# Attention experts: eight keys and values projected first, and five passes instead of six

## The reference

```
def _expert(x, Wqkv, bqkv, Wo, bo, g1, be1, W1, bf1, W2, bf2, g2, be2):
    q, k, v = split(x @ Wqkv.T + bqkv)          # 8 heads of 64
    attn = softmax((q / 8) @ k.T, axis=-1)      # over all 128 nodes
    ctx = (attn @ v) @ Wo.T + bo
    x = layernorm(x + ctx, g1, be1)
    h = gelu(x @ W1.T + bf1)                    # 512 -> 64
    h = gelu(h @ W2.T + bf2)                    # 64 -> 512
    return layernorm(x + h, g2, be2)

probs = softmax((x @ gate_Wk.T + gate_bk) @ expert_queries.T * D ** -0.5)
gated = probs of the top 2 of 8 experts, over their sum + 1e-9, 0 for the others
out = sum over e of gated[:, e] * _expert(x, e)
```

## Time and profile before

| | |
|---|---|
| three timed runs | 439.18, 439.82, 439.83 us, median 439.82 |
| the profiled execution | 439.57 us, of which the span is 437.8 |
| PE busy | 408.1 us, 93% of the span |
| DVE, ACT, POOL busy | 47%, 30%, 9% |
| attention experts, from the first q matmul to the sum written to x | 167.2 to 319.0 us |

### The profile page before, as it was taken

One profiled execution on the slowest core, in us unless ns is written; L12 is line 12 of the kernel. 1 busy time (PEld: TensorE's weight loads), 2 busy tenths in 40 slices (PEclk: granted clock), 3 DMA queues, 4 the chain that ended last, 5 costly groups with the idle time before them and its releaser, 6 DMA issues.

```text
span 437.8 us, 7601 instructions
## 1 busy us (share of the span) xinstructions
PE 408.1 (93%) x2811; PEld 308.5 (70%) x2811; DVE 207.6 (47%) x598; ACT 131.3 (30%) x382; POOL 40.9 (9%) x80
## 2 busy tenths in 40 slices
PE   7998999896499989999999999998999999999996
PEld 6698655885098789797685669656788995393482
DVE  5743554555994254562745547557442621111102
ACT  2313322414562112351533235342112231222130
POOL 4000010011453011001000010001010000000000
PEclk9999999999769999999999999999999999999999
DMA  8999569322002200999999999337200499999900
GB/s 288 394 426 354 217 248 398 145 98 96 0 2 97 97 0 2 370 393 422 416 320 313 358 422 306 95 122 310 104 0 0 192 418 425 421 418 421 390 5 24
DMA packets 19494, 104.31 MB, mean 238 GB/s; under 512 B 3538, under 2 KB 5458, under 8 KB 7809
## 3 DMA queue, kind: packets, MB, share of 16 engines
q1 hardware_dynamic: 19168, 103.81, 61.7%
q10 hardware_dynamic: 288, 0.02, 0.1%
HBM read 103.56 MB, written 0.26 MB: 237 GB/s over the span
## 4 chain that ended last, share of the span: by engine, by line
PE 52%; issue 4%; DVE 2%; DMA 1%; ACT 1%; POOL 0%; SPq 0%; POOLq 0%; DVEq 0%; ACTq 0%
PE ps L1186 9%; PE ps L1172 8%; PE ps L1855 6%; PE ps L1589 6%; PE ps L1578 3%; PE ps L1569 3%; PE ps L1672 3%; DMA ew<-in_l_wq 1%; PE ps L1206 1%; PE ps L1693 1%; PE ps L1921 1%; PE ps L1702 1%; PE ps L1197 1%; PE ps L1216 1%; PE ps L1155 1%
## 5 line engine op out<-in xcount | busy, mean ns | idle before, releaser
L1155 PE MATMUL ps<-ident 128*128 128x128 f32 x352 | 48.8, 292 | 2.8 <-POOL ident L664 2.8
L1155 PEld LDWEIGHTS ps<-ident 128*128 128x128 f32 x352 | 46.3, 207 | 5.0 <-POOL ident L664 2.8
L1186 PEld LDWEIGHTS ps<-y_t,ew 128*128 128x128 f32 x352 | 39.9, 192 | 1.7 <-issue 1.7
L1186 PE MATMUL ps<-y_t,ew 128*128 128x128 f32 x352 | 40.2, 275 | 0.0
L1172 PE MATMUL ps<-ew,y_t 128*128 128x512 f32 x72 | 32.7, 597 | 0.0
L1589 PE MATMUL ps<-y_t,ew 128*128 128x128 f32 x224 | 27.5, 277 | 0.0
L1589 PEld LDWEIGHTS ps<-y_t,ew 128*128 128x128 f32 x224 | 26.1, 192 | 0.8 <-issue 0.7
L813 ACT ACTIVATE prob_store<-ps,nmax_s 128x128 f32<-128x128 f32 x56 | 19.7, 384 | 14.5 <-DVE nmax_s L2047 14.5
L1172 PEld LDWEIGHTS ps<-ew,y_t 128*128 128x128 f32 x72 | 13.0, 190 | 13.5 <-issue 13.3
L2655 DVE SCALAR_TENSOR_TENSOR t<-prob_store 128x512 f32<-128x512 f32 x6 | 4.2, 692 | 36.4 <-ACT prob_store L1089 20.4
L749 POOL TENSOR_TENSOR ln_rstd<-ln_mv,minus_half 128x1 f32<-128x1 f32 x12 | 6.6, 549 | 127.7 <-DVE ln_mv L2409 127.7
(11 more groups left out here) (529 smaller groups left out, 759.4 us busy)
## 6 DMA issues: line engine op xcount, KB each, us to landing
ew<-in_l_w SPq DMA_DIRECT2D x20, 1024.0 KB, 21.5
dense<-in_l_w SPq DMA_DIRECT2D x12, 1024.0 KB, 21.1
ew<-in_l_wv SPq DMA_DIRECT2D x8, 1024.0 KB, 14.8
ew<-in_l_wk SPq DMA_DIRECT2D x7, 1024.0 KB, 15.3
ew<-in_l_wq SPq DMA_DIRECT2D x6, 1024.0 KB, 11.8
erows<-in_l_rows SPq DMA_DIRECT2D x4, 1280.0 KB, 12.8
ew<-in_l_wo SPq DMA_DIRECT2D x5, 1024.0 KB, 14.8
ew<-in_gqa_wq SPq DMA_DIRECT2D x3, 1024.0 KB, 10.5
```

The lines of the kernel that those rows point to most:

```text
L1155: pe.matmul(ps[:, b, 3 * P:4 * P], ident[:], ident[:], start=True, stop=True)
L1186: last = pe.matmul(ps[:, b, m * n:(m + 1) * n], w[:, c, (first + m) * P:(first + m + 1) * P], in_t[:, c, 0:n], start=(c == 0), stop=(c == ...
```

## The change

All eight keys come first, then all eight values, each in the order of the experts' own numbers, so none of them waits for the ranking. Their results stay in `k_all` and `v_all` (four slots of `dense`), and GpSimd copies those of a pass's experts into the tiles that the matmuls read (`keys_copy`, `values_copy`). All eight experts are ranked. Ranks 0 and 1 have passes of their own, the first and the last; ranks 2 and 7 share one in groups of 96 and 32 slots, ranks 3 and 4, and 5 and 6, share one each in halves. [...]

With no projections of keys and values left beside the passes, `beside_pair` holds the steps of pass t, the gather, the q and its turning for pass t+2, and the scores. The value's bias moves behind the attention (`v_bias` now adds it to the transposed context, since the weights of a row sum to one), and that copy out of PSUM moves from ScalarE to VectorE. The key's bias moves from VectorE to ScalarE. The last two passes are interleaved by hand. GCN's weights no longer load into `dense` ahead of the stage, but into `ew` during the passes.

```
-L2_STEPS = ((0,), (1,), (2, 3), (4,), (5, 6), (7,))
-L2_RANKS = (None, 0, 3, 4, 1, 5, 6, 2)
+L2_STEPS = ((0,), (1, 2), (3, 4), (5, 6), (7,))
+L2_RANKS = (0, 2, 7, 3, 4, 5, 6, 1)
+L2_PAIRS = (1, 2, 3)
+L2_SPANS = {1: (slice(0, 96), slice(96, P)), 2: (slice(0, 64), slice(64, P)), 3: (slice(0, 64), slice(64, P))}
+L2_GROUPS = {1: ((0, 0, 64), (0, 64, 96), (1, 96, P)), 2: ((0, 0, 64), (1, 64, P)), 3: ((0, 0, 64), (1, 64, P))}
...
             def load_l2_rows(t, experts):
+                for r, e in zip(L2_SPANS[t] if t in L2_PAIRS else (slice(0, P),), experts):
+                    sp.dma_start(erows[r, t % 2], A["l2_rows"][e].rearrange("(a r) n -> a r n", a=1)
+                                 .broadcast_to([r.stop - r.start, 4, D])).then_inc(sig(f"l2_rows_landed{t % 2}"), 16)
...
             sp.wait_ge(*at("l2_expert_added", 1))
+            load_l2_rows(2, (e3, e4))
...
+            def keys_copy(t):
+                pool.wait_ge(*at("l2_k_ready", E))
+                if t:
+                    pool.wait_ge(*at("l2_scored", 2 * t))
+                for a, p in enumerate(L2_STEPS[t]):
+                    pool.tensor_copy(keys_of[a].rearrange("p c n -> p (c n)"),
+                                     k_all[:, bass.ds(experts[p], 1), :].rearrange("p e n -> p (e n)")) \
+                        .then_inc(sig("l2_k_copied"), 1)
+
+            def values_copy(t):
+                pool.wait_ge(*at("l2_v_ready", E))
+                if t:
+                    pool.wait_ge(*at("l2_attended", t))
...
+            keys_copy(0)
+            keys_copy(1)
+            values_copy(0)
+
+            keys_copy(2)
+            values_copy(1)
+            inner_norm(0, 1)
...
+            def on_groups(t, b, in_t, kind, columns=slice(0, D), started=False):
+
+                for c in range(CH):
+                    for a, first, end in L2_GROUPS[t]:
+                        last = pe.matmul(ps[first:end, b, 0:columns.stop - columns.start], in_t[:, c, first:end],
+                                         l2_w(kind, L2_STEPS[t][a])[:, c, columns],
+                                         start=(c == 0 and not started), stop=(c == CH - 1))
+                return last
...
             def beside_pair(t):
 
-                first, second = L2_STEPS[t + 2]
-                step_attend(t, 7)
+                step_attend(t, 1)
                 gather_rows(t + 2)
                 step_o(t)
-                expert_k(first, range(CH))
                 pair_q(t + 2)
                 x1_transposes(t)
-                expert_k(second, (0, 1))
+                turn_q(t + 2)
                 step_h1(t)
-                turn_q(t + 2)
-                expert_k(second, (2, 3))
+                probs_t(t + 1)
                 step_h2(t)
-                probs_t(t + 1)
-                step_v(t + 1)
                 step_scores(t + 2)
...
+            for e in range(2, 7):
+                expert_k(e)
+            expert_q(0)
+            expert_k(7)
+            expert_v(0)
             step_scores(0)
+            expert_v(1)
+            gather_rows(1)
+            expert_v(2)
+            pair_q(1)
+            expert_v(3)
+            turn_q(1)
             probs_t(0)
+            for e in range(4, E):
+                expert_v(e)
             step_scores(1)
+
             beside_pair(0)
-            beside_dense(1)
-            beside_pair(2)
-            beside_dense(3)
+            beside_pair(1)
...
+            step_attend(2, 1)
+            keep_clock(2, times=2)
+            step_o(2)
+            expert_q(4)
+            x1_transposes(2)
+            turn_scatter()
+            step_h1(2)
+            probs_t(3)
+            step_h2(2)
+            step_scores(4)
+
+            step_attend(3, 1)
+            keep_clock(2, times=2)
+            step_o(3)
+            keep_clock(2, times=8)
+            probs_t(4)
+            x1_transposes(3)
+            step_attend(4, 0)
+            step_h1(3)
+            step_o(4, (0,))
+            step_h2(3)
+            step_o(4, (1,))
```

More of the change, by code:

```diff
@@ L1631, in step_scores @@
                 for g in range(4):
-                    for a, r in enumerate(token_half):
-                        for rows, keys in zip(token_half, (qk_t[:, CH:], k_second)):
-                            last = pe.matmul(ps[rows, 3 + a, g * P:(g + 1) * P], qk_t[r, g, rows], keys[r, g, :],
-                                             start=True, stop=True)
+                    for h, r in enumerate(token_half):
+                        for a, first, end in L2_GROUPS[t]:
+                            last = pe.matmul(ps[first:end, 3 + h, g * P:(g + 1) * P], qk_t[r, g, first:end],
+                                             keys_of[a][r, g, :], start=True, stop=True)
                         if g == 3:
@@ L1651, in step_attend @@
                 pe.wait_ge(*at("l2_prob_t_ready1", t + 1))
-                for rows, values in zip(token_half, (v, v_second)):
+                for tokens, values in zip(L2_SPANS[t], values_of):
                     for g in range(4):
@@ L1778, in _ @@
+            step_h1(2)
[13 more added lines that the diff above has]
+            step_o(4, (1,))
             pe.wait_ge(*at("l2_scatter_ready", 1))
             pe.matmul(bank(2), gated_t[:], be2[:], start=True, stop=False)
-            pe.matmul(bank(2), scatter[:, 0:P], pair_rows[0], start=False, stop=False)
@@ L1781, in _ @@
-            keep_clock(1, times=6)
-            pe.wait_ge(*at("l2_expert_added", 5))
-            pe.matmul(bank(2), scatter[:, P:2 * P], pair_rows[1], start=False, stop=True).then_inc(sig("l2_mixed"), 1)
-            x1_transposes(5)
+            for k in range(2):
+                pe.matmul(bank(2), scatter[:, k * P:(k + 1) * P], pair_rows[k], start=False, stop=False)
+            keep_clock(1, times=4)
+            x1_transposes(4)
             keep_clock(1, times=3)
-            step_h1(5)
@@ L1787, in _ @@
-            keep_clock(1, times=2)
-            step_h2(5)
+            step_h1(4)
+            pe.wait_ge(*at("l2_expert_added", LAST))
+            pe.matmul(bank(2), scatter[:, 2 * P:3 * P], pair_rows[2], start=False, stop=True).then_inc(sig("l2_mixed"), 1)
+            step_h2(4)
             gcn_out = ((4, 5), (6, 7), (0, 3))
@@ L2402, in statistics @@
-            def statistics(rows):
-                settle()
-                dve.bn_stats(ln_st[:, 0:6], rows[:])
-                aggregate(ln_st[:])
+                dve.wait_ge(*at("l2_attended", t + 1))
+                for tokens, p in zip(L2_SPANS[t] if t in L2_PAIRS else (slice(0, P),), L2_STEPS[t]):
+                    last = dve.tensor_tensor(ctx_t[:, :, tokens], bank_chunks(0 if t == LAST else 1)[:, :, tokens],
+                                             bqk[:, bass.ds(experts[p] * 12 + 2 * CH, CH)].unsqueeze(2)
+                                             .broadcast_to([P, CH, tokens.stop - tokens.start]), ALU.add)
@@ L2407, in aggregate @@
+                last.then_inc(sig("l2_ctx_t_ready"), 1)
+            rows_landed = (16, 32, 48, 64)
             def aggregate(stats):
@@ L2589, in _ @@
-            keep_pair(4)
-            first_norm(5)
+            experts = [expert_at(p) for p in range(E)]
+            v_copy(0)
+            weights_max(0)
+            v_copy(1)
+            weights(0, (0,))
+            v_copy(2)
+            weights(0, (1,))
+            v_copy(3)
+            pair_q_bias(1)
+            prob_t_copy(0)
+            for e in range(4, E):
+                v_copy(e)
+            weights_max(1)
+            v_bias(0)
+            first_sums(0)
+            first_norm(0)
```

800 lines of the change are left out of this document (384 added, 416 removed), and 7 rows, old and new, of the table L2_LOADS.

## The result

The change made the kernel slower: 460.16 us (458.71 to 461.33, four runs) against 439.82 in the same comparison, a ratio of 1.046 (95% interval 1.043 to 1.050). The forecast was 434.8 and its range ended at 447.5.

What follows compares the result with a forecast made beforehand. TensorE was taken to bound the stage, busy 150.07 of 151.80 us. 8.6 us less work, about 3.6 back as waits, made the stage 146.8, 5.0 less: 434.8 us in all, range 432.5 to 447.5.

Steps and rivals of the forecast that it cites:

- first rival: Pair of 96 and 32: groups of 64, 32 and 32 rows don't overlap; 12.3 us more, 447.1; chance 0.28.
- the sentence on SP: SP's queue: loads behind the wait to load pass 2's bias rows; none wanted within 10 us.
- no wait exceeds 2 us: Passes: argument against TensorE getting a lower clock; late rows or lower clock gave 438 to 445, waits' chance 0.10.
- the sum said: Whole stage, front through tail: 146.8 us against 151.8 before, 5.0 less.
- front and first pass: Keys, values, first q and scores, 69.0 us without waits; then the first expert pass, 14.9.
- the second pass: Pass of 96 and 32 slots, priced as a pair of halves plus small steps and waits: 16.4 us.
- the third: Third expert pass, with dummies, value bias, last expert's q and scatter transposes: 16.2 us.
- the tail: Stage end, from the fourth pass's attention to the sum written to x: 30.3 us.
- the interleaved part: Tail: dummies, weights, x1, then attention, output halves and second MLP matmul in turn: 11.6 us, 1.8 held by VectorE.
- the last chain: End of the tail, first norm through MLP, scatter and Gelu to x; nothing shortens it: 12.0 us.
- rival of dear copies: GpSimd's copies of values and keys take 2.4 us each, losing the gain: 439.5 us; chance 0.10.
- third pass's rows of biases: Loads wanted some 6.4 us after their buffer frees; fit narrowly, costing 1 us per us late.

Runs made afterwards that it cites:

- last version: Changed kernel with four groups of 32 rows, last three passes' small loads before most GCN/LSTM weights, last bias rows also before the second GCN load: 437.37 us.
- the control: Kernel before the change, with only the second half of each of its two pairs cut into two groups of 32 rows: 473.64 us, ratio 1.076.

## Why the prediction was wrong

**The step that failed** is the choice between forecast and first rival: that a 64-row matmul runs beside two of 32 rows, so that the pair of 96 and 32 costs what a pair of halves costs. The rows ahead of the change showed the gap at each change of width, and the prediction named it, but took it as no evidence on overlap. Measured by itself, with the lower clock behind its scores, the mix is worth 18.4 us (460.16 - 441.72), and 16.8 per pair in a kernel without the change. That rival was the mechanism, and its price of 12.3 was low mainly by one term: q 4.3 extra (4.2 said), output projection 5.4 (5.0), second MLP matmul 1.0 (1.05), scores 5.6 where 2 was taken between 1.1 and 4. In the scores not only 64 and 32 but also the two heads of a chunk, which run side by side where all groups have one size, follow one another: eight times 0.70 us where 1.1 was said for all, which is 4.5 extra, and the lower clock adds the other 1.1. With 16.3 for 12.3 the rival would have said 451; the rest of the way to 460 is the late weights and the clock, which it did not hold, and no case's range reached 460.

The Trainium skill, "TensorEngine Tiling (Array Packing)", section Tiling Modes, says that a change of the tiling mode drains TensorE and that different tiles can work in parallel. By both, four groups of 32 can run together and 64 beside 32 can't, and the traces agree (q 3.6 us and 7.9).

**The second step that failed** is what the sentence on SP was taken to show: that of the loads queued behind the wait for the first expert's sum "none is wanted within 10 us", so that they come in time. The sentence itself held: in the change the sum let SP go on at 282.88, and the small weights of the third pass were wanted at 297.2. What it left out is the 3 MB ahead of them; the matmul could start only at 298.73. With the groups of one size, taking such waits away was worth 3.8 us (441.72 - 437.90). Most of it lies in the third pass, which takes 20.0 us with the small weights late and 16.5 with all of them ahead: 1.9 of waiting and 1.6 at the lower clock behind it.

**The clock** was weighed with the argument that no wait exceeds 2 us. It fell behind one wait (2.54 us, then 0.52 for 6.6 us) and not behind the one of 2.41, and before both with no wait at all, in the mixed scores. In the run with all four groups of 32 it fell twice, first behind a wait of 2.86 us and then again near 300 us:

```profile
282.51 0.69 PE L1733 MATMUL ps<-x_t,ew 128*64 128x64 f32 x16 [2.86 <-DMA gat_rows<-in_l_w]
```
```profile
283.00:287.00 4.00, 4.00 (x23) 1.99 (x21) 1.04 (x2) 1.21 (x3) 0.00 (x0) 0.57 0.89 211
300.30:303.60 3.30, 3.16 (x33) 2.94 (x34) 0.69 (x1) 0.96 (x3) 0.00 (x0) 0.55 1.01 382
```

Shortly ahead of the second fall no wait was longer than 1.06 us. The last version has the same waits at that place (0.17, 1.06 and 0.21 us), and its clock stayed at 1.00:

```profile
294.00:305.00 11.00, 9.12 (x64) 5.73 (x63) 5.68 (x12) 2.42 (x5) 1.81 (x2) 1.00 0.84 338
```

So the longest wait did not decide whether the clock fell; what does was not settled.

**What was right.** With both causes taken away, the stage of the last version, which starts at 167.09, runs as the sum said, except for 2.7 us: front and first pass take 250.86 - 167.09 = 83.8 (69.0 + 14.9 = 83.9 said), the second pass 17.1 (16.4; the scores wait 0.94 for VectorE's q bias), the third 16.5 (16.2), the tail 32.1 (30.3; the fourth pass 7.1 for 6.7, the interleaved part 12.3 for 11.6, the last chain 12.7 for 12.0). That is 149.5 against 146.8, and against 151.8 before. GpSimd's copies take 0.61 us, inside the bounds of 0 to 2.4 and below the 1.0 that was taken; TensorE waited 0.48 for the first where 0.7 was said. A row of GpSimd's timeline in the change:

```profile
240.02 0.61 POOL L777 COPY v<-dense 128x512 f32 x1 [34.03 <-DVE dense L2430]
```

The rival of dear copies has a sum that does not come out: 3.8 - 0.6 + 1.0 gives 439.0, with the 1.4 added 440.4, and 439.5 was written. Nothing hangs on it, as the copies were cheap.

The third pass's rows of biases, which were to cost 1 us for each us of delay, were late in the change: VectorE's first half of the sum waited for them until 289.85, some 0.7 us after the matmuls that it reads had ended. This cost nothing, since the second half, whose matmuls ended later, could start without delay.

So the pass that goes is worth about 2.4 us, half of what was said, and only if the pair of 96 and 32 is cut evenly and the small loads come ahead.

## What to carry to other kernels

Give matmuls that are to run side by side one tile size: here 96 + 32 ran in the time of a pair of halves when cut into four 32s, and not as 64 + 32 + 32. Price an uneven mix as a sequence until a run shows otherwise. Where work leaves the critical engine, list for each small load how many MB stand ahead of it in its queue at the time when its buffer comes free; large loads for a later stage belong behind the small ones that the next step wants. Moving one late load ahead shows its value only when the next one in the queue is also in time.

## What the runs showed of the hardware

- Matmuls of 64 and of 32 rows did not overlap, and a change between them cost about 0.13 us besides; four of 32 rows took no longer than two of 64 (q 3.6 us).
- TensorE's clock fell to the lower level with TensorE busy throughout, in scores that went by 64 and 32 in turns: in the change (0.54 over 7.1 us) and in the control (0.65 over 9.7 us). It did not fall behind 8 us of q in the same turns, nor in scores of one size. What sets the scores apart was not settled.
- GpSimd copies 128x512 float32 in 0.61 us, as long as it takes for a 128x128 scaling, and about half as long as an addition of the same shape.
